# Router scores and gates turned by VectorE in 32x32 blocks instead of by TensorE

## The reference

```
scores = xf @ Wr.T                      # 1024 tokens x 64 experts
top_vals, top_idx = top_k(scores, 16)
gates = softmax(top_vals)
G[token, top_idx] = gates               # 0 for the other 48
h = einsum('nd,krd->nkr', xf, A)
out = einsum('nkr,kdr->nd', h * G[:, :, None], B) * 2
```

## Time and profile before

| | |
|---|---|
| time, median of 3 runs | 355.08 us (354.74 to 355.09) |
| profiled execution, its own time | 354.69 us |
| span of its instructions | 353.0 us |
| PE busy | 349.5 us (99%) |
| DVE busy | 202.2 us (57%) |
| ACT busy | 144.1 us (41%) |
| POOL busy | 78.0 us (22%) |
| granted TensorE clock, mean | 1.0 |

### The profile page before, as it was taken

The page is one execution under the profiler, slowest core; times in us unless marked ns, Lnnn a source line. Parts: engine busy times, 40 slices in busy tenths (PEclk is TensorE's granted clock), DMA queues, the critical chain, the costliest instruction groups (busy, mean ns, idle before and its releaser), DMA issues.

```text
span 353.0 us, 4621 instructions
## 1 busy us (share of the span) xinstructions
PE 349.5 (99%) x1682; PEld 294.4 (83%) x1682; DVE 202.2 (57%) x302; ACT 144.1 (41%) x196; POOL 78.0 (22%) x86
## 2 busy tenths in 40 slices
PE   8999999999999999999999999999999999999997
PEld 8899888888888888888888898888888888888885
DVE  3788755334533453685674565879888878501102
ACT  5577544422442243545464471566352443201100
POOL 2361657863340004000000000000041154002200
PEclk9999999999999999999999999999999999999999
DMA  7943343232120054297219019010052022101011
GB/s 202 323 126 144 114 138 112 78 104 77 52 80 0 0 177 130 79 395 291 59 35 306 3 22 417 38 52 11 0 177 62 0 61 69 51 32 59 30 61 59
DMA packets 14802, 37.31 MB, mean 106 GB/s; under 512 B 2272, under 2 KB 4224, under 8 KB 13504
## 3 DMA queue, kind: packets, MB, share of 16 engines
q1 hardware_dynamic: 11920, 31.18, 25.9%
q0 software_dynamic: 2432, 5.57, 5.5%
q10 hardware_dynamic: 432, 0.33, 0.3%
HBM read 34.97 MB, written 2.10 MB: 105 GB/s over the span
## 4 chain that ended last, share of the span: by engine, by line
PE 99%; DVE 0%; issue 0%
PE ps L1157 29%; PE ps L1158 29%; PE ps L1159 29%; PE ps L1179 3%; PE ps L1309 3%; PE ps L1399 1%; PE ps L1386 1%; PE ps L1194 1%; PE ps L1187 1%; PE ps L1198 1%; PE ps L1202 1%; PE ps L1234 1%; PE ps L1408 0%; PE ps L1417 0%; DVE x L1149 0%
## 5 line engine op out<-in xcount | busy, mean ns | idle before, releaser
L1158 PE MATMUL ps<-x_hl,w_hl 128*128 128x512 f32 x144 | 56.2, 390 | 0.0
L1157 PE MATMUL ps<-x_hl,w_hl 128*128 128x512 f32 x144 | 56.2, 390 | 0.0
L1159 PE MATMUL ps<-x_hl,w_hl 128*128 128x512 f32 x144 | 56.1, 389 | 0.0
L462 POOL TENSOR_TENSOR am_hl<-am_raw,am_hl 128x512 fp32r<-128x512 f32 x8 | 11.0, 1387 | 137.4 <-ACT am_hl L479 137.4
L418 POOL DMA_INDIRECT b_raw<-b_gu,row_of x32 | 32.1, 1003 | 27.7 <-DVE b_st L780 19.6
L800 DVE TENSOR_TENSOR glu<-glu,ps 128x512 f32<-128x512 f32 (+1 forms) x22 | 14.9, 683 | 38.8 <-ACT glu L511 26.0
L1159 PEld LDWEIGHTS ps<-x_hl,w_hl 128*128 128x128 f32 x144 | 27.1, 188 | 5.7
L511 ACT ACTIVATE glu<-ps 128x512 f32<-128x512 f32 (+1 forms) x22 | 12.8, 588 | 46.0 <-PE ps L1179 45.8
L1157 PEld LDWEIGHTS ps<-x_hl,w_hl 128*128 128x128 f32 x144 | 27.1, 188 | 5.4
L1158 PEld LDWEIGHTS ps<-x_hl,w_hl 128*128 128x128 f32 x144 | 27.1, 188 | 5.2
L1158 PE MATMUL ps<-act,wd_hl 128*128 128x512 f32 x80 | 31.2, 390 | 0.0
(11 more groups left out here) (151 smaller groups left out, 729.0 us busy)
## 6 DMA issues: line engine op xcount, KB each, us to landing
wc_raw<-mask_w SPq DMA_DIRECT2D x8, 1024.0 KB, 7.0
w_raw<-w_gu SPq DMA_DIRECT2D x8, 512.0 KB, 3.3
wd_raw<-w_dn SPq DMA_DIRECT2D x10, 256.0 KB, 2.7
w_raw<-w_t SPq DMA_DIRECT2D x2, 1024.0 KB, 7.3
x<-x_blocks SPq DMA_DIRECT2D x2, 1024.0 KB, 6.3
am_raw<-a_moe SPq DMA_DIRECT2D x8, 256.0 KB, 2.8
bm_raw<-b_moe SPq DMA_DIRECT2D x4, 512.0 KB, 3.6
x_raw<-x_blocks SPq DMA_DIRECT2D x7, 256.0 KB, 6.7
```

Source lines behind the costliest of these rows:

```text
L462: nc.gpsimd.tensor_tensor(am_hl[:, j % AM_SLOTS, 1], am_raw[:, j % 2], am_hl[:, j % AM_SLOTS, 0].bitcast(F32), ALU.subtract).then_inc(am_l ...
L1157: nc.tensor.matmul(out, w_high, m_high, start=start, stop=False)
L1158: nc.tensor.matmul(out, w_high, m_low, start=False, stop=False)
L1159: return nc.tensor.matmul(out, w_low, m_high, start=False, stop=stop)
```

## The change

Scores: ScalarE copies only partitions 64 to 127 of bank 4 to `s_sb`. VectorE adds partitions 0 to 63 of the bank to them, and turns the 64x512 sum by eight instructions, each of which takes 32 partitions and 128 elements (four blocks of 32x32) to 32 other partitions of `score`. Gates: VectorE scales them once per expert (one `scalar_tensor_tensor` in place of four `tensor_scalar`), and turns them by eight such instructions straight into the lower half of `gate_x`; ScalarE copies that to the upper half. TensorE's `turn_scores` and `turn_gates` go, and with them `ident2` in the constants (464 to 400 columns).

Order: at row 6 of the `cond` loop VectorE turns the scores of half 0 where it ran `route_first8(0)`, which now follows `ct_low(7)`. Ahead of `hg_gate(0)` it turns those of half 1, and `route_first8(1)` follows `hg_gate(1)`. On ScalarE `exponent(0)` moves behind `am_high(2)` and `am_high(3)`. `scores(1)` waits for VectorE's sum of half 0, since that now reads bank 4.

```diff
@@ ScalarE
             def s_copy(s):
                 act_e.wait_ge(s_ready, s + 1)
-                copy(s_sb[:], ps[:, 4]).then_inc(s_copied, 1)
+                copy(s_sb[EXPERTS:P], ps[EXPERTS:P, 4]).then_inc(s_copied, 1)
...
             def gate_copy(s):
-                act_e.wait_ge(gate_tr, s + 1)
-                copy(gate_x[:, s], ps[:, 6]).then_inc(late_banks_free, 2)
+                act_e.wait_ge(gate_turned, s + 1)
+                copy(gate_x[EXPERTS:P, s], gate_x[0:EXPERTS, s]).then_inc(late_banks_free, 2)
...
             ct_high(BATCH - 1)
-            exponent(0)
             am_high(2)
             am_high(3)
+            exponent(0)
@@ VectorE
+            def turn_scores(s):
+                dve.wait_ge(s_copied, s + 1)
+                nc.vector.tensor_tensor(s_sb[0:EXPERTS], ps[0:EXPERTS, 4], s_sb[EXPERTS:P], ALU.add).then_inc(s_summed, 1)
+                dve.wait_ge(s_summed, s + 1)
+                for e in range(0, EXPERTS, BLOCK):
+                    summed = s_sb[e:e + BLOCK].rearrange("p (t q n) -> p t q n", t=4, n=BLOCK)
+                    for q in range(P // BLOCK):
+                        last = nc.vector.transpose(score[q * BLOCK:q * BLOCK + BLOCK, :, e:e + BLOCK], summed[:, :, q])
+                step(last)
+
             def route_first8(s):
-                dve.wait_ge(score_ready, s + 1)
-                step(nc.vector.tensor_copy(score[:], ps[:, 5, 0:4 * EXPERTS].rearrange("p (t e) -> p t e", t=4)))
...
                 step(nc.vector.reciprocal(gate_inv[:], gate_sum[:]))
-                if s:
-                    dve.wait_ge(gate_tr, s)
-                for t in range(4):
-                    last = nc.vector.tensor_scalar(
-                        gate2[:, t], left1[:, t].unsqueeze(1).broadcast_to([P, 2, EXPERTS]),
-                        gate_inv[:, t:t + 1], MOE_SCALE, ALU.mult, ALU.mult)
-                last.then_inc(gate_done, 1)
+                step(nc.vector.scalar_tensor_tensor(gate_tok[:], left1[:], MOE_SCALE,
+                                                    gate_inv[:].unsqueeze(2).broadcast_to([P, 4, EXPERTS]),
+                                                    ALU.mult, ALU.mult))
+                for e in range(0, EXPERTS, BLOCK):
+                    turned = gate_x[e:e + BLOCK, s].rearrange("p (t q n) -> p t q n", t=4, n=BLOCK)
+                    for q in range(P // BLOCK):
+                        last = nc.vector.transpose(turned[:, :, q],
+                                                   gate_tok[q * BLOCK:q * BLOCK + BLOCK, :, e:e + BLOCK])
+                last.then_inc(gate_turned, 1)
...
                 if b == 6:
-                    route_first8(0)
+                    turn_scores(0)
             ct_low(BATCH - 1)
+            route_first8(0)
             route_next8()
             route_gates(0)
...
-            route_first8(1)
+            turn_scores(1)
             hg_gate(0)
             hg_gate(1)
+            route_first8(1)
             hg_low(0)
@@ TensorE
             def scores(s):
...
+                if s:
+                    pe.wait_ge(s_summed, s)
...
                 turn(b - 1)
-                if b == 6:
-                    turn_scores(0)
...
             experts(1)
-            turn_scores(1)
-            turn_gates(0)
...
             experts(5)
-            turn_gates(1)
...
-                    pe.wait_ge(late_banks_free, 2 * o + s + 1)
+                    pe.wait_ge(late_banks_free, max(4, 2 * o + s + 1))
```

More of the change, by code:

```diff
@@ L70 @@
 AM_SLOTS = 4
+BLOCK = 32
 H_ORDER = [(j + dj, s) for j in range(0, JT, AM_SLOTS) for s in range(2) for dj in range(AM_SLOTS)]
@@ L96, in build @@
         assert base + R_ACT + 88 * KB <= nc.sbuf_usable_end
-        const_sb = at("const_sb", [P, 464], F32, R_CONST)
+        const_sb = at("const_sb", [P, 400], F32, R_CONST)
         block_mask = const_sb[:, 0:PAIR]
         ident = const_sb[:, PAIR:PAIR + P]
[L101 to L105, removed]
+        bias0_sb = const_sb[:, PAIR + P:PAIR + P + KD]
+        lora_w_sb = const_sb[:, PAIR + P + KD:PAIR + P + KD + 1]
+        coeff_sb = const_sb[:, PAIR + P + KD + 1:PAIR + P + KD + 1 + BATCH]
+        small = R_CONST + 400 * 4
         small_sb = at("small_sb", [P, 64], I32, small)
@@ L176, in build @@
         expo = at("expo", [P, 4, EXPERTS], F32, R_AD + 15 * KB)
-        gate2 = at("gate2", [P, 4, 2, EXPERTS], F32, R_ACT + 54 * KB)
+        gate_tok = at("gate_tok", [P, 4, EXPERTS], F32, R_ACT + 54 * KB)
         gate_x = at("gate_x", [P, 2, HALF], F32, R_AD)
@@ L232, in build @@
         wr_hi, wr_lo = sem("wr_hi"), sem("wr_lo")
-        s_ready, s_copied, score_ready = sem("s_ready"), sem("s_copied"), sem("score_ready")
-        top_step, shifted, exp_done, gate_done = sem("top_step"), sem("shifted"), sem("exp_done"), sem("gate_done")
-        gate_tr, late_banks_free = sem("gate_tr"), sem("late_banks_free")
+        s_ready, s_copied, s_summed = sem("s_ready"), sem("s_copied"), sem("s_summed")
+        top_step, shifted, exp_done = sem("top_step"), sem("shifted"), sem("exp_done")
+        gate_turned, late_banks_free = sem("gate_turned"), sem("late_banks_free")
         am_hi, am_lo, h_ready, hg_mul, hg_hi, hg_lo = (sem("am_hi"), sem("am_lo"), sem("h_ready"), sem("hg_mul"),
@@ L299, in _ @@
                 load_a(b, dma_a[1])
-            sp.dma_start(const_sb[:, PAIR:464], consts[:, PAIR:464]).then_inc(dma_const, 16)
+            sp.dma_start(const_sb[:, PAIR:400], consts[:, PAIR:400]).then_inc(dma_const, 16)
             def load_tile(f, slot):
@@ L1402, in scores @@
                 last.then_inc(s_ready, 1)
[L1404 to L1419, removed]
             def experts(n, part=range(KD)):
@@ L1491, in constants @@
     eye = np.eye(P)
-    return np.concatenate([LORA_SCALE * own, eye, eye[:, :EXPERTS] + eye[:, EXPERTS:]], 1).astype(np.float32)
+    return np.concatenate([LORA_SCALE * own, eye], 1).astype(np.float32)
 def rows_of_tiles():
@@ L1558 @@
         "b_moe": a["L1_ffn_B"].transpose(2, 0, 1).reshape(JT, P, KD, P).transpose(2, 1, 0, 3),
-        "consts": columns(464, [constants(), a["L0_ffn_bias"].reshape(KD, P).T,
+        "consts": columns(400, [constants(), a["L0_ffn_bias"].reshape(KD, P).T,
                                 np.repeat(a["L0_ffn_lora_weights"], RANK).reshape(P, 1),
```

## The result

The changed kernel takes 360.4 us (360.05 to 361.4, 6 runs) beside 354.91 us for the kernel before on the same chip: a ratio of 1.0157, interval 1.0146 to 1.0167. It is 5.5 us slower. Its profiled execution took 360.05 us with a span of 358.3, against 354.69 and 353.0 before, so the profile has 5.3 of the 5.5 to explain.

A forecast was written before the change was run, and what follows sets the result against it. TensorE bounds the kernel, but VectorE's queue to hg_gate(3) grows 8.0 us, so experts(7) starts 4.4 and experts(8) 4.7 later: 354.69 becomes 359.4, plus 0.4 for the median, 359.8 us; range 355.6 to 363.4.

The forecast's parts named there:

- What leaves TensorE: TensorE's score and gate turns go, taking 2.7 us off it; with full cover the kernel would gain just that.
- The price of a turn: Each of 32 block turns on VectorE costs 0.31 us, 9.9 in all; bounds 0.20 and 0.45 each.
- The pair of the earlier trace: At 150.08 on VectorE, the second instruction reads another group of 32 partitions in PSUM; the two take 0.86 us, without overlap.
- Its other pair: Two VectorE instructions of 256 elements, said to stay in one group of 32 partitions, overlap and take 0.75 us.
- the rival of dear turns: Block turns on VectorE cost 0.40 us and more, giving up to 364.3 us; chance 0.13.
- The rest of VectorE's queue: VectorE from the end of ct_low(5) to hg_gate(3): with the turns and all other items the sum is +8.0 us.
- The idle time that stays: Of VectorE's 1.9 us of idle time before hg_gate(3), about 0.8 stays, so -1.1.
- the subtraction beside `am_low`: On VectorE, the subtraction ahead of the exponent now meets GpSimd's am_low, for about +0.5 us.
- TensorE's waits: New TensorE idle times at the last turn and ahead of experts(4), experts(6), experts(7); not added up, the last sets the time.
- The tail over ScalarE and GpSimd: gate_copy(1) and am_high(4) follow hg_high(3), so GpSimd's am_low(4) ends late and experts(8) starts 4.7 us later.
- The rival of the clock and of GpSimd: Idle times lower TensorE's clock, or am_low holds half 0's turns: 1.3 to 3.6 us more, 361.1 to 363.4; chance 0.15.
- The rival on the other side: Faster than before through VectorE's slack ahead of experts(7), if a turn costs under 0.16 us; chance 0.10.

The follow-up runs named there:

- scores_by_scalar: gates_only with hg_low(2), hg_gate(3) ahead of route_gates(1), am_high(4) ahead of gate_copy(1), and half 1's turned scores copied by ScalarE; 353.86 us, 0.9965.
- same_rows: Changed kernel with every block turn reading and writing partitions 0 to 31, most experts' scores and gates left out; 356.95 us, 1.0049.
- experiment 4: Changed kernel with route_first8(0) back behind turn_scores(0), ahead of c_bias(7); its run is first8_early; 361.77 us, 1.0187.
- experiment 2: Changed kernel with each set of eight block turns done twice, with a wait between; its run is double_turns; 371.37 us, 1.0474.
- experiment 5: Changed kernel with am_high(4) ahead of gate_copy(1) on ScalarE; its run is am_first; 360.35 us, 1.0155.
- gates_only: Kernel before with only the gates scaled and turned by VectorE as in the change, scores still turned by TensorE; 355.43 us, 1.0007.
- am_first: Run of experiment 5: changed kernel with am_high(4) ahead of gate_copy(1) on ScalarE; 360.35 us, 1.0155.
- first8_early: Run of experiment 4: changed kernel with route_first8(0) back behind turn_scores(0), ahead of c_bias(7); 361.77 us, 1.0187.
- double_turns: Run of experiment 2: changed kernel with each set of eight block turns done twice, with a wait between; 371.37 us, 1.0474.

## Why the prediction was right

The forecast was 359.8 us, and 360.4 was measured. By its steps:

- **What leaves TensorE**, 2.7 us: the instructions of L1408 and L1417 are gone. That it is worth something where VectorE has room is seen in scores_by_scalar, which has 0.94 of it. Its `experts(0)` starts 0.05 later than in the kernel before and its `experts(8)` 0.85 earlier, and its span is 0.9 shorter; the medians differ by 1.1.
- **The price of a turn**, which decided: 0.315 measured, 0.31 forecast, so 10.1 instead of 9.9 us. The pair of the earlier trace rows had it: an instruction that touches another group of 32 partitions waits for the end of the one before. same_rows shows that this is the cause and not only a fitting number. But the reason given, that each block turn writes to another group than the one before it, holds for the score turns alone. Six of the eight gate turns of a set write to the same group as the one before and only read another. By writes alone they would have overlapped, so that the price held for them too is partly luck, though the pair in the earlier trace rows is itself one that differs in what it reads. Its other pair spans all 128 partitions; what it keeps is the first partition, and not one group of 32. The duration, 0.30, is 0.02 over the 0.28 of the earlier trace rows, so gathering 32 columns costs next to nothing, and the rival of dear turns falls. By the Trainium skill's figure (VectorE: DVE Perf Modes, "The three transpose paths") a block turn of 128x128 bf16 takes 311 ns; the trace has 302 for 32x128 fp32. The Trainium skill's section "Two Vector instructions with no wait between them" of the same page says that an instruction is also held back when an input starts in another group than the one last read in the same memory. The traces agree: about 0.315 apart with either group changed, 0.19 to 0.24 with neither.
- **The rest of VectorE's queue**: +8.0 forecast to `hg_gate(3)`, 286.59 - 278.43 = 8.16 measured, of which 0.1 was there at the end of `ct_low(5)`. (The eight `tensor_scalar` of the earlier trace rows are 2.0, not 1.9.) The idle time that stays was put at 0.8 and is 0.78; the subtraction beside `am_low` at +0.5 and is 0.90 instead of 0.43. Not foreseen was 0.29 of idle VectorE ahead of `hg_low(0)`, which waits for ScalarE.
- **TensorE's waits**: forecast 1.5, some 2, 1 and 2.6 us; measured 1.48, 1.79, 0.85 and 2.33. That the early ones don't add up was right in direction (experiment 4), with a reservation for the clock.
- **The tail over ScalarE and GpSimd** was the term that was sized too small. `experts(8)` was forecast 0.3 us behind the end of `experts(7)`, at +4.7; it is at +5.25. 0.2 of it is `hg_gate(3)`. Most of the rest stands in ScalarE's timeline of the changed kernel, against the earlier trace rows:

```profile
286.63 0.63 ACT L479 ACTIVATE hg<-hg_raw 128x512 fp32r<-128x512 f32 x1 [4.69 <-DVE hg_raw L1125]
287.28 0.63 ACT L479 ACTIVATE gate_x<-gate_x 64x512 f32<-64x512 f32 x1
287.94 0.63 ACT L479 ACTIVATE am_hl<-am_raw 128x512 fp32r<-128x512 f32 x1
```

The copy starts 0.65 after the instruction before it and the next 0.66 after the copy; between the copy from PSUM and `am_high(4)` before it was 0.50. I had taken 0.5 for both. The new copy writes from partition 64 on, the others from 0. It also reads SBUF instead of PSUM, but that is not the reason, as `s_copy(0)` shows, which reads PSUM in both kernels. Before, where it takes all partitions, and after, where it takes 64 to 127:

```profile
251.81 0.60 ACT L479 ACTIVATE c_hl<-ps 128x512 fp32r<-128x512 f32 x1 [1.56 <-PE ps L1386]
252.30 0.59 ACT L479 ACTIVATE s_sb<-ps 128x512 f32<-128x512 f32 x1
...
251.82 0.60 ACT L479 ACTIVATE c_hl<-ps 128x512 fp32r<-128x512 f32 x1 [1.56 <-PE ps L1398]
252.45 0.59 ACT L479 ACTIVATE s_sb<-ps 64x512 f32<-64x512 f32 x1
```

The distance grows from 0.49 to 0.63.
- **The rival of the clock and of GpSimd** did not come: the granted clock is 1.00 from 260 to 295 in the profiled execution of the changed kernel, and the turns of half 0, which lie beside GpSimd's `am_low`, stand 0.315 apart like the others. The clock is real, though, as experiments 2, 4 and 5 show. In the changed kernel's other runs it may add to the spread: the longest, of 359.7, has 0.995. But one of 359.0 has 1.0, so the spread has another part too, and what made the median's rise a little larger than the profile's stays open.
- **The rival on the other side**, faster if a turn costs under 0.16, was well placed: at 0.19 to 0.24 in same_rows the kernel is still 0.5% slower.

## What to carry to other kernels

Before moving work from the engine that is 99% busy to one at 57%, count the second one's queue in the stretch where it happens, up to the instruction that the first will ask for: here the slack was 3.6 us and the net work 8. A part of such a change can pay where the whole does not, since slack is spent once; half of the idea with two moves in the order and one copy given to ScalarE beat both kernels. A block turn on VectorE should be priced as an instruction that can't overlap its neighbour, when it reads or writes another group of 32 partitions than the neighbour does.

## What the runs showed of the hardware that I had not expected

- VectorE holds a turn back for a change of the group that it reads as much as for one of the group that it writes: 0.315 apart in the gate sets and in the score sets of the changed kernel alike, 0.19 to 0.24 where neither changes (same_rows). Not being held also shortens the record of a turn, from 0.30 to 0.26.
- ScalarE, too, starts an instruction only after the end of the one before it where the first partition changes: 0.65 and 0.66 from start to start for 0.63 of duration, against 0.50 for 0.60. It shows in the changed kernel and in gates_only (282.53 and 283.19). That the source is SBUF does not explain it: `s_copy(0)` reads PSUM and stands 0.63 instead of 0.49 behind its neighbour, and in am_first `am_high(4)` follows `hg_high(3)`, both from SBUF and from partition 0, by 0.54. No run separates the first partition from the number of partitions, which is 64 in each held copy.
- The granted TensorE clock fell behind idle times of 1.80 us (am_first) and 2.35 us (first8_early), and did not behind 1.79 and 2.33 us in the changed kernel's profile. The same kernel has runs with and without it. A fall lasted some 3.5 us in am_first; its price was nothing where TensorE waited again before the last wait, and about 1 us behind the last one (first8_early, double_turns).
